# Moving the first two chunks' activations ahead of the router's softmax, and two gated sums behind the third chunk's second layer, in the last stage of a two-layer kernel

## The reference, cut to what matters

```
xr = layernorm(x).reshape(-1, D)                    # 2048 x 256
route_probs = softmax(xr @ wr.T, axis=-1)           # 8 experts
routes_k, indices_k = top_k(route_probs, 2)
gates = routes_k / sum(routes_k, axis=-1, keepdims=True)
h = silu(xr @ w1.T); h = silu(h @ w3.T); h = h @ w2.T
out = zeros_like(xr)
for k in range(2):
    out = out.at[indices_k[:, k]].add(gates[:, k:k+1] * h)
x = x + out
```

## Time and profile before

| | |
|---|---|
| median of 3 runs | 1221.81 us (1221.64 to 1226.63) |
| the profiled execution: span from first to last instruction | 1222.5 us (no time of its own is given beside the span) |
| PE busy | 1090.1 us, 89% |
| DVE busy | 916.0 us, 75% |
| ACT busy | 623.8 us, 51% |
| mean granted TensorE clock | 0.953 |
| last stage (PE's first matmul of it to the end) | 1164.96 to 1222.5 us |

### The profile page before, as it was taken

How to read it: one execution, slowest core, us unless ns; L and a number is a source line. 1 busy time by engine, 2 the same in 40 slices (tenths; PEclk the granted TensorE clock), 3 DMA queues, 4 the chain that set the end, 5 groups by cost and what they waited for, 6 DMA issues and landing times. The chain is left out here.

```text
span 1222.5 us, 18399 instructions
## 1 busy us (share of the span) xinstructions
PE 1090.1 (89%) x7034; PEld 752.9 (62%) x7034; DVE 916.0 (75%) x1702; ACT 623.8 (51%) x1092; POOL 218.6 (18%) x173
## 2 busy tenths in 40 slices
PE   2969999999999998877877989999996999999978
PEld 2823333333333346666666768888885889899866
DVE  7778999999999824488898886555553878897832
ACT  2525878878788763766641233333334333433323
POOL 6004500000000001000034203000001744744300
PEclk9959999999999999888988989999997899999989
DMA  2880232143030000000000021011001000000010
GB/s 95 198 258 18 37 54 39 16 54 53 2 54 2 2 1 31 1 1 0 1 18 1 1 91 35 18 35 35 18 1 61 2 1 1 1 1 1 1 66 5
DMA packets 24850, 40.02 MB, mean 33 GB/s; under 512 B 3116, under 2 KB 12344, under 8 KB 24760
## 3 DMA queue, kind: packets, MB, share of 16 engines
q1 hardware_dynamic: 24760, 38.82, 13.7%
HBM read 28.06 MB, written 10.49 MB: 32 GB/s over the span
## 5 line engine op out<-in xcount | busy, mean ns | idle before, releaser
L721 DVE TENSOR_REDUCE att_mx<-att_ps_m 128x2 f32<-128x1024 f32 x256 | 310.9, 1225 | 25.1 <-PE att_ps_m L587 21.5
L698 ACT ACTIVATE att_prob<-att_ps_s 128x512 f32<-128x512 f32 x512 | 278.2, 596 | 89.9 <-PE att_ps_s L637 77.9
L653 PE MATMUL att_ps_o<-att_prob,v_rows 128*32 128x256 f32 (+1 forms) x1920 | 159.4, 405 | 0.0
L1931 POOL TENSOR_TENSOR qry_prod<-qry_qr,lin_ksum 128x512 f32<-128x512 f32 x64 | 92.9, 1452 | 303.0 <-ACT qry_qr L2052 288.9
L637 PE MATMUL att_ps_s<-qst,kst 50*128 50x512 f32 x512 | 128.0, 496 | 11.0 <-ACT att_prob L698 10.4
L637 PEld LDWEIGHTS att_ps_s<-qst,kst 50*128 50x128 f32 x512 | 48.1, 183 | 123.7 <-ACT att_prob L698 114.2
L587 PE MATMUL att_ps_m<-kst,qst 48*128 48x512 f32 x512 | 110.6, 427 | 9.0 <-DVE att_mx L721 6.9
L2052 ACT ACTIVATE qry_qr<-qry_ps_q 128x512 f32<-128x512 f32 x64 | 38.3, 598 | 132.9 <-PE qry_ps_q L153 124.0
L153 PE MATMUL qry_ps_o<-qry_m,qry_n_hi 128*128 128x256 f32 x512 | 99.7, 293 | 0.4 <-DVE qry_n_lo L1961 0.3
L1642 DVE SCALAR_TENSOR_TENSOR key_k_lo<-kf_ps,key_k_hi 128x512 fp32r<-128x512 f32 x64 | 44.2, 691 | 61.6 <-ACT key_k_hi L1720 61.0
L653 PEld LDWEIGHTS att_ps_o<-att_prob,v_rows 128*32 128x32 f32 x1920 | 38.1, 108 | 84.7 <-ACT att_prob L698 71.1
(11 more groups left out here) (425 smaller groups left out, 2336.8 us busy)
## 6 DMA issues: line engine op xcount, KB each, us to landing
qst<-qk_parts SPq DMA_DIRECT2D x48, 128.0 KB, 4.7
kst<-qk_parts SPq DMA_DIRECT2D x48, 128.0 KB, 7.3
qk_parts<-att_out SPq DMA_DIRECT2D x16, 256.0 KB, 5.6
qk_parts<-qk_lo SPq DMA_DIRECT2D x16, 256.0 KB, 5.8
residual<-L_attn_x SPq DMA_DIRECT2D x4, 512.0 KB, 6.1
lin_wq_raw<-L_attn_Wv SPq DMA_DIRECT2D x4, 512.0 KB, 3.7
lin_wq_raw<-L_attn_Wq SPq DMA_DIRECT2D x4, 512.0 KB, 5.3
lin_wq_raw<-L_attn_Wo SPq DMA_DIRECT2D x4, 512.0 KB, 3.9
```

What stands on the lines that cost most here:

```text
L653: ins = nc.tensor.matmul(ps_o[32 * h:32 * h + 32, cols], vall[:, NS * b + s, h0 + h, :], prob[:, u % PR, h, cols], start=s == 0, stop=s == ...
L698: nc.scalar.activation(prob[:, u % PR, 2 * j + r, :], ps_s[:, (n + r) % BANKS, :], ACT.Exp).then_inc(exp_ok, 1)
L721: nc.vector.reduce_max(mx[:, v % 2, :, m], ps_m[:, n % 2], AX.X).then_inc(m_rd, 1)
L1931: nc.gpsimd.tensor_tensor(prod[:, u % 2, :], qr[:, u % 2, :], ksum[:, b, cols(n)], ALU.mult).then_inc(pr_ok, 1)
```

## The change

On DVE, `low_h(0)` and `low_h(1)` now stand ahead of the router's maximum, `low_h(2)` behind `shares`, and `low_h(3)` behind the gates. On ACT, the one-column Exp is gone; `layer1(0)` and `layer1(1)` stand ahead of the Exp on the logits, and the rest keeps its order. On PE, the gated sums of chunks 0 and 1 stand together behind layer 2 of chunk 2; those of chunks 2 and 3 stay behind layer 2 of chunk 3. From the Exp on, line numbers are up to four higher.

```diff
--- before.py
+++ after.py
@@ -2283,16 +2283,16 @@
                 dve.wait_ge(iota_ok, 1)
                 nc.vector.tensor_copy(iota_f[:], iota_i[:])
                 last_low()
+                low_h(0)
+                low_h(1)
                 dve.wait_ge(l_ps, d.NC)
                 link(nc.vector.tensor_reduce(lmax[:], ps_l[:], AX.X, ALU.max))
                 nc.vector.tensor_tensor(lg[:], ps_l[:], spread(lmax[:], NE), ALU.subtract).then_inc(lmax_ok, 1)
                 shares()
-                low_h(0)
+                low_h(2)
                 places()
-                low_h(1)
                 gates()
-                for c in range(2, d.NC):
-                    low_h(c)
+                low_h(3)
                 dve.wait_ge(a_ps, 1)
                 nc.vector.tensor_copy(acc[:], ps_a[0:NE, 0:d.E]).then_inc(acc_ok, 1)
                 dve.wait_ge(a_ps, 2)
@@ -2307,9 +2307,6 @@
                 for k in range(d.KT):
                     act.wait_ge(t_ps, k + 1)
                     nc.scalar.activation(turned_rows(d, keep, 0, k, LAST * d.CH, d.CH), ps_2[:, k, :], ACT.Copy).then_inc(hi_ok, 1)
-                nc.scalar.activation(warm[:], w.sd[:, 0:1], ACT.Exp, scale=0.0).then_inc(warm_ok, 1)
-                act.wait_ge(lmax_ok, 1)
-                nc.scalar.activation(ex[:], lg[:], ACT.Exp).then_inc(ex_ok, 1)
 
                 def layer1(c):
                     for m in range(d.KT):
@@ -2329,10 +2326,15 @@
                             .then_inc(h2_ok, 1)
 
                 layer1(0)
-                for c in range(d.NC):
-                    if c + 1 < d.NC:
-                        layer1(c + 1)
-                    layer2(c)
+                layer1(1)
+                act.wait_ge(lmax_ok, 1)
+                nc.scalar.activation(ex[:], lg[:], ACT.Exp).then_inc(ex_ok, 1)
+                layer2(0)
+                layer1(2)
+                layer2(1)
+                layer1(3)
+                layer2(2)
+                layer2(3)
 
             @block.tensor
             def _(pe):
@@ -2416,9 +2418,11 @@
                     if 2 <= c + 1 < d.NC:
                         layer1(c + 1)
                     layer2(c)
-                    if c:
-                        add_up(c - 1)
-                add_up(d.NC - 1)
+                    if c == d.NC - 2:
+                        for i in range(c):
+                            add_up(i)
+                for c in (d.NC - 2, d.NC - 1):
+                    add_up(c)
                 pe.wait_ge(acc_ok, 1)
                 for k in range(d.KT):
                     ins = nc.tensor.transpose(flat_l[:, k * NE:(k + 1) * NE], acc[:, k * P:(k + 1) * P],
```

## The result

The changed kernel takes 1215.41 us (median of four runs, 1214.22 to 1216.97) against 1223.14 us for the kernel before beside it (four runs, 1221.64 to 1226.63). The ratio is 0.9945, with a 95% interval of 0.9924 to 0.9965: faster by 4 to 9 us, most likely 6.7. Timed again later it was 0.9949 (0.9932 to 0.9966).

The account below looks back on a forecast made before the run. PE's 5.50 us wait for `rt_h_lo` ahead of layer 2 of chunk 0 was taken as the bound in the last stage. Gains of 5.74 + 0.41 + 0.22 = 6.37 us took 1221.81 to 1215.4 us, range 1213.5 to 1218.0.

Parts of the forecast that it names:

- everything behind it: PE behind layer 2 of chunk 0: moving chunk 0's gated sum saves two changes of matmul kind, 0.22 us.
- The margins: Last stage: gates 1.8 us early for the sums, layer 2 of chunk 1's Silu 2.9 us early.
- the third part pays for the second: PE's gated sums: in its old place chunk 0's sum would wait 3.8 us for the later gates; moved, it does not.
- parts 1 and 2: ACT and DVE: first activations ahead of the router's softmax, router behind them; layer 2 5.74 us earlier and 0.41 us shorter.
- part 3: PE: gated sum of chunk 0 moved from between layer 2 of chunk 1 and layer 1 of chunk 3; 0.22 us gained.
- part 2: DVE and ACT: router behind the first activations, gates 2.4 us later, added Exp load taken to cost 0 us.
- The first: Rival, PE's restart at layer 2 of chunk 0: clock stays low longer, gain 4.6 us, 1217.2 us; chance 15%.
- Its 7.0 us end: Longest low-clock stretch allowed from layer 2's start, from PE busy at the low level without a gap; costs 1.75 us.
- The second: Rival, ACT: a switch of tables costs 1.38 us more than its row, gain 5.2 us, 1216.6 us; chance 7%.
- The third: Rival: layer 2 of chunk 0 still waits for the router or another semaphore, about 1 us gained, 1220.8 us; chance 6%.
- The fourth: Rival, PE from layer 2 of chunk 0: clock low for all the rest, slower, 1237.8 us; chance 3%.

Follow-up runs that it names:

- e1: The changed kernel with PE's gated sums back in their old places, DVE and ACT as changed; ratio to the kernel before 1.0000.
- e3: The changed kernel with PE's gated sums in their old places and DVE's low parts of chunk 2 behind the gates; ratio to the kernel before 0.9943.
- e0: The changed kernel timed again without an edit; ratio to the kernel before 0.9949.
- e5: The changed kernel with the one-column Exp put back ahead of layer 1, one more change of tables; ratio to the kernel before 0.9958.
- e6: The changed kernel with seven wide layer 1 matmuls held back from between the router's matmuls to behind the last chunk's turn; ratio to the kernel before 0.9977.
- e4: The changed kernel with PE's turn of the last chunk's tokens ahead of the router's third chunk; ratio to the kernel before 0.9918.
- e8: The changed kernel with the last chunk's turn ahead of the router's third chunk, timed a second time; ratio to the kernel before 0.9905, 1211.76 us.
- e7: The changed kernel, last chunk's turn ahead of the router's second chunk, layer 2 of chunk 0 begun between the router's last tiles; ratio to the kernel before 0.9907.

## Why the prediction was right

Predicted 1215.4, measured 1215.41. So close a hit is luck, as the kernel before moved by 1.3 us between its two medians; the ratio's interval is what it should be held against, and 6.4 us of gain lies within 4 to 9. The profile tests the terms better:

| step | predicted | measured |
|---|---|---|
| layer 2 of chunk 0 starts earlier (in the stage's own time) | 5.74 us | 26.43 to 20.86: 5.57 us |
| layer 2 of chunk 0 is shorter | 0.41 us | 4.80 to 4.20: 0.60 us |
| everything behind it | 0.22 us | 21.66 to 21.37: 0.29 us |
| sum | 6.37 us | 6.46 us |

Of the 0.17 us missing in the first term, 0.10 are the step from narrow to wide: 0.21 us at the low clock, where I took the 0.11 that the narrow matmuls have at the full one. The other 0.07 lie in the router, whose last matmul starts 20.65 us into the stage and not 20.58. The second is the low stretch: 2.9 us where I took 3.5 from two restarts.

The margins came as worked out, too. With the stage shifted by 0.89 us, the gates end at 1199.39 (1199.4 predicted); the sums stand 1.8 us behind them; layer 2 of chunk 1 could have started 2.9 us earlier as far as its Silu is concerned. The Exp load did not wait for the Exp's semaphores, as the earlier trace rows had shown of another load.

The sentence that "the third part pays for the second" was right and too mild. It named a wait of 3.8 us; e1 shows 3.7 us and then a clock that falls, so parts 1 and 2 without part 3 give nothing. It took the price for a given, though: e3 shows that the wait came from where part 2 put the low parts of chunk 2, and that with the gates first nothing has to be paid for.

**The rivals.** The first (low clock for longer) did not decide the result, but it is real: the low stretch from the start of layer 2 was 2.9, 2.6 and 6.0 us in the changed kernel, e0 and e1, whose order is the same up to there (and 5.9 us in e5), so a single execution moves by up to 1.7 us. Its 7.0 us end was not reached. The second (tables cost 1.38 us more) is out by e5. The third is out: the wait is gone. The fourth, the slower one, is out, since the clock rose 2.9 us into layer 2. Yet dense work following narrow work directly was a sound worry: PE's mixture of mostly narrow matmuls brings the clock down by itself (e6), without any idle time. What I had of it was right (layer 2 of chunk 0 inherits the low clock from the router). What I believed of its cause until e4 (the 1.57 us wait) was half right: the wait brings the fall forward into the router's last chunk, and without it the clock falls in layer 2 (e4, e8).

## What to carry to other kernels

When a wait on PE is released by a chain through several engines, check which links need one another and which only stand in one queue; here the router's softmax stood ahead of activations that were ready. When you move work ahead, ask what on the same engine moves behind an instruction that waits for PE: the gates cost 3.7 us plus a fallen clock in e1, and either moving their user (the change) or moving the waiting instruction behind them (e3) mends it. And look at what PE does, not only whether it is busy: mixing narrow matmuls with wide ones made the profiled stage 1.5 us shorter in e7 with the same instructions, though the times are too coarse to show it.

## What the runs showed of the hardware that I had not expected

- The granted clock was at 0.54 in the mean over 11 us in which PE was busy without a gap, with one 512-column matmul to six 8-column ones (e6); with two to six it stayed at 1.00 for 14 us (e4, e7).
- Narrow matmuls alone ran at 1.00 for 3.2 us behind busy work (e4, e8), and the clock fell only in the dense matmuls behind them; behind an idle stretch of 1.57 us it fell after 0.64 us of them (the changed kernel).
- An idle stretch of 3.73 us at the full clock costs more than itself: the clock fell 0.9 us after work resumed, and the sum and the 12 matmuls behind it took 1.7 us longer (e1).
- An ACT_TABLE_LOAD runs ahead of the wait of the activation it serves (1185.48 against 1186.72 in the changed kernel) and costs 1.28 us and no more (e5). That it does not wait was expected from the earlier trace rows; that nothing else comes with it had been open.
